# The last stage of a four-stage transformer kernel: who computes its gates, routing factors and roots, and in which order

## The reference, cut to what matters

```python
x = x + wkv(layernorm(x), ctx)              # stage 1
x = x + quantised_ffn(layernorm(x))         # stage 2
x = x + cross_attention(layernorm(x), ctx)  # stage 3: 8 groups x 2 heads
x = x + L1_ffn(layernorm(x))                # stage 4

def L1_ffn(x):                              # the sequence is the BATCH axis: l = 4 positions
    x = silu(x_prev * conv_w[:, 0] + x * conv_w[:, 1])
    q, k, v, g = silu(x @ Wq), x @ Wk, x @ Wv, x @ Wg       # 16 heads, 8 and 16 wide
    q, k = rotary(q), rotary(k)
    scores = softmax(v @ router_w)                          # 2 routes
    onehot = one_hot(argmax(scores))
    norm = 1 / cumsum(onehot over positions)
    qk = (q * scores * onehot * norm) . (k * onehot) * 8 ** -0.5, causal
    o = qk @ v
    o = (o - mean(o)) / sqrt(var(o) + 1e-5)                 # per head, 16 wide
    return (silu(g) * o) @ Wout
```

## Time and profile before

| | |
|---|---|
| median of 3 timed runs | 670.36 us (670.31 to 671.44) |
| the profiled execution's own time | 670.83 us |
| its span in the trace | 668.9 us |
| busy over the span | PE 92%, DVE 79%, ACT 60%, POOL 38% |
| mean granted TensorE clock | 0.987 of full |

### The profile page before, as it was taken

The page is one execution under the profiler, slowest core; times in us unless marked ns, Lnnn a source line. Parts: engine busy times, 40 slices in busy tenths (PEclk is TensorE's granted clock), DMA queues, the critical chain, the costliest instruction groups (busy, mean ns, idle before and its releaser), DMA issues.

```text
span 668.9 us, 13295 instructions
## 1 busy us (share of the span) xinstructions
PE 613.5 (92%) x4567; PEld 491.5 (73%) x4567; DVE 531.4 (79%) x1305; ACT 398.9 (60%) x1339; POOL 256.0 (38%) x338
## 2 busy tenths in 40 slices
PE   4556999999999999999999999999999999999937
PEld 3445787777778887778788877877888888767725
DVE  6998687988897778888877788888664777778797
ACT  4367766666776645667566456585663655655531
POOL 2215664444333454343335443333332444430233
PEclk9998999999999999999999999999999999999987
DMA  8475742424533202233342223332252323010001
GB/s 273 146 276 195 240 161 61 126 91 91 187 144 103 102 12 103 102 104 104 107 138 90 83 103 104 103 104 103 104 171 97 103 103 103 17 33 1 1 0 63
DMA packets 36973, 72.86 MB, mean 109 GB/s; under 512 B 3343, under 2 KB 28587, under 8 KB 32811
## 3 DMA queue, kind: packets, MB, share of 16 engines
q1 hardware_dynamic: 36720, 72.00, 32.9%
q10 hardware_dynamic: 186, 0.02, 0.0%
HBM read 59.41 MB, written 12.60 MB: 108 GB/s over the span
## 4 chain that ended last, share of the span: by engine, by line
PE 63%; DVE 21%; issue 7%; POOL 5%; ACT 4%; DMA 1%; SPq 0%; DVEq 0%; POOLq 0%
PE bank L718 13%; PE bank L698 11%; PE bank L587 10%; PE bank L594 6%; PE bank L670 5%; PE bank L742 3%; PE bank L684 3%; PE bank L699 3%; POOL rs L1351 2%; ACT square L1089 2%; DVE nm L1768 2%; DVE Cb L1783 2%; PE bank L834 2%; PE bank L732 1%; PE bank L843 1%
## 5 line engine op out<-in xcount | busy, mean ns | idle before, releaser
L718 PEld LDWEIGHTS bank<-V,Pt 128*128 128x128 f32 x1024 | 128.1, 191 | 29.1 <-DVE Cb L1783 15.3
L1089 ACT ACTIVATE square<-bank 128x128 bf16<-128x128 f32 x372 | 97.9, 280 | 85.0 <-PE bank L587 71.1
L718 PE MATMUL bank<-V,Pt 128*128 128x129 f32 x1024 | 136.3, 276 | 3.4 <-DVE Cb L1783 3.2
L698 PE MATMUL bank<-QT,KTt 128*128 128x512 f32 x256 | 132.6, 599 | 2.7 <-POOL diag L1366 2.7
L1366 POOL TENSOR_TENSOR diag<-identb,nm 128x512 bf16<-128x512 bf16 x64 | 66.9, 1045 | 173.3 <-DVE nm L1768 173.2
L1072 ACT ACTIVATE Pt<-bank 128x512 f32<-128x512 f32 x128 | 76.8, 600 | 65.4 <-PE bank L699 62.1
L1768 DVE TENSOR_REDUCE nm<-bank 128x2 f32<-128x512 f32 x128 | 82.4, 685 | 25.6 <-PE bank L684 25.2
L1351 POOL TENSOR_TENSOR rs<-ve,mhalf 128x6 f32<-128x6 f32 x64 | 90.0, 1406 | 5.3
L1783 DVE SCALAR_TENSOR_TENSOR Cb<-bank,ro,ism 128x128 bf16<-128x128 f32 x256 | 78.1, 347 | 4.5
L587 PE MATMUL bank<-WQ,xq 128*128 128x256 f32 x512 | 79.4, 297 | 1.5 <-DVE xq L1679 1.4
L1089 ACT ACTIVATION_READ_ACCUMULATOR square<-bank 128x1 f32 x372 | 78.0, 210 | 0.0
(11 more groups left out here) (233 smaller groups left out, 1021.1 us busy)
## 6 DMA issues: line engine op xcount, KB each, us to landing
WQ<-wq_split SPq DMA_DIRECT2D x24, 1024.0 KB, 7.7
WH<-wh_split SPq DMA_DIRECT2D x24, 384.0 KB, 8.9
wq_split<-WQ SPq DMA_DIRECT2D x8, 1024.0 KB, 5.4
ism<-smooth_inverse SPq DMA_DIRECT2D x32, 256.0 KB, 6.4
wpst<-in_L_xattn_wproj SPq DMA_DIRECT2D x16, 256.0 KB, 4.6
wh_split<-WH SPq DMA_DIRECT2D x8, 384.0 KB, 4.0
wst<-in_L_xattn_wq SPq DMA_DIRECT2D x8, 256.0 KB, 5.0
wst<-in_L_xattn_wqx SPq DMA_DIRECT2D x8, 256.0 KB, 5.2
```

Source lines behind the costliest of these rows:

```text
L698: nc.tensor.matmul(o[:], KTt[u % 2][:, x, t * P:(t + 1) * P], QT[u % 2][:, x, :], start=True, stop=False)
L718: last = nc.tensor.matmul(o[:, h * (P + 2):h * (P + 2) + P + 1], Pt[:, x, k, h * S + t * P:h * S + (t + 1) * P], V[u % 2][:, x, k, 0:P + 1 ...
L1089: last = A(square[:, t, h], head(t, h), ACT.Square, accum_out=ss[:, t, h:h + 1])
```

## The change

Everything is in the tail; the 31 units before it keep their code, apart from the products of three head groups of `project_last`, put into unit 30.

- **TensorE:** `project_last` goes by head groups. Group 0, then 1 and 2, of tile 0 move into unit 30; the transposes of inputs stand between the last `weigh`s. Tile 0 and tile 1 post `proj_done` each for itself. Keys and gates of a tile are separate steps with semaphores of their own (`qkv3_evac`, `g3_evac`); for the last two tiles the gates come first. PSUM banks are given out anew.
- **ACT:** `turned3` takes silu straight from PSUM for l = 0 and multiplies by the convolution's second weight for the others; hT is copied for l = 0 to 2 only. The tanh is taken beside the gate's evacuation, from PSUM (`gates3`). The roots take 1/16 and eps by scale and bias. A new `gate3(l)`, for l = 0 and 1, makes the gate product of a batch as 32 activations of 128 x 16, each with its own per-partition scale out of `r3`; both stand right behind the root over l = 0 to 2, ahead of turned 0, squares3(3), turned 1, the last root and turned 2.
- **DVE:** `convolve3` keeps one operation for each column half; `route3` makes the whole factor `wt` (routes, counts, score) before `dots3`, which multiplies once. `head_rstd3` moves ahead of the sum in `dots3(3)`. The tensor_scalar of `variance3` and `weigh3` of l = 0 to 2 go.
- **GpSimd:** it gets `weigh3(0)`, `(1)` and `(2)`, between the rotations; the rotation of l = 3 is done tile by tile (twelve operations instead of six); it keeps `gate3(2)` alone.

```diff
+        eps = sb("eps", [P, 1])
+            chain.add(gp.memset(eps[:], EPS))
...
                 weigh(u, 1, 1)
+                if u == UNITS - 2:
+                    project_last(0, (0,))
                 guard(u + 1, 1)
+                if u == UNITS - 2:
+                    project_last(0, (1, 2))
...
             weigh(u, 0, 1)
+            turn_inputs3(0)
             weigh(u, 1, 0)
+            turn_inputs3(1)
             weigh(u, 1, 1)
-            for l in range(B - 1):
-                turn_inputs3(l)
-            project_last(0, True)
+            turn_inputs3(2)
+            project_last(0, (3, 4, 5, 6))
+            project_last(1, (0, 1, 2, 3))
             turn_outputs(u)
-            project_last(1, True)
-            project_last(0, False)
-            project_last(1, False)
-            project3(0)
+            project_last(1, (4, 5, 6))
+            project_last(0, (7,))
+            project_last(1, (7,))
+            for m in range(NT):
+                project3_keys(m)
+                project3_gate(m)
             turn_inputs3(B - 1)
-            for l in range(1, B):
-                project3(l)
+            for m in range(NT, T8 - NT):
+                project3_keys(m)
+                project3_gate(m)
+            for m in range(T8 - NT, T8):
+                project3_gate(m)
+            for m in range(T8 - NT, T8):
+                project3_keys(m)
...
+            def gates3(m):
+                act.wait_ge(s["gate3_done"], m + 1)
+                l, t = divmod(m, NT)
+                B_ = P3B[m % 2]
+                A(dl[:, l, t * H3:(t + 1) * H3], B_[:, D:D + H3], ACT.Copy)
+                A(cf[:, l, t * H3:(t + 1) * H3], B_[:, D:D + H3], ACT.Tanh, scale=0.5)
+                A(g3[:, m, :], B_[:, 0:D], ACT.Silu).then_inc(s["g3_evac"], 1)
+
+            def gate3(l):
+
+                if l == 0:
+                    act.wait_ge(s["head_rstd_ready"], 1)
+                    act.wait_ge(s["og_ready"], B - 2)
+                for n in range(NT * H3):
+                    last = A(heads(o3, l)[:, n], heads(g3, l)[:, n], ACT.Copy, scale=r3[:, l, n:n + 1])
+                last.then_inc(s["o_ready"], 1)
...
             squares3(2)
             act.wait_ge(s["sd_ready"], B - 1)
-            A(r3[:, 0:B - 1], m3[:, 0:B - 1], ACT.Sqrt).then_inc(s["sd_done"], 1)
+            A(r3[:, 0:B - 1], m3[:, 0:B - 1], ACT.Sqrt, scale=1.0 / DV3, bias=eps[:]).then_inc(s["sd_done"], 1)
+            gate3(0)
+            gate3(1)
             turned_outputs3(0)
+            squares3(B - 1)
             turned_outputs3(1)
-            squares3(B - 1)
+            act.wait_ge(s["sd_ready"], B)
+            A(r3[:, B - 1], m3[:, B - 1], ACT.Sqrt, scale=1.0 / DV3, bias=eps[:]).then_inc(s["sd_done"], 1)
             turned_outputs3(2)
-            act.wait_ge(s["sd_ready"], B)
-            A(r3[:, B - 1], m3[:, B - 1], ACT.Sqrt).then_inc(s["sd_done"], 1)
...
+            def weigh3(l):
+
+                pool.wait_ge(s["sq_ready"], l + 1)
+                pool.wait_ge(s["g3_evac"], NT * (l + 1))
+                gp.tensor_tensor(rows3(g3, l), rows3(g3, l), rows3(o3, l), ALU.mult).then_inc(s["og_ready"], 1)
...
             power3(B - 1, B, 2)
-            for l in range(1, B):
-                rotate3(l)
-            for l in range(B - 1):
-                gate3(l)
+            weigh3(0)
+            rotate3(2, NT, 1)
+            rotate3(4, NT, 2)
+            weigh3(1)
+            rotate3(6, 1, 3)
+            rotate3(7, 1, 4)
+            weigh3(2)
+            gate3(2)
...
             def route3(l):
 
-                dve.wait_ge(s["qkv3_evac"], 3 * NT * (l + 1))
...
+                dve.wait_ge(s["g3_evac"], NT * m)
+                ch.add(v.tensor_scalar(sel[:, l], dl[:, l], 0.0, None, ALU.is_ge))
+                link(v.scalar_tensor_tensor(out=cf[:, l], in0=cf[:, l], scalar=-1.0, in1=cf[:, l], op0=ALU.mult, op1=ALU.max))
...
+                w = wt[:, 0:m, :]
+                link(v.tensor_tensor(w, sel[:, 0:m, :], sel[:, l:l + 1, :].to_broadcast([P, m, n3]), ALU.is_equal))
+                link(v.tensor_reduce(cnt[:], w.rearrange("p m n -> p n m"), AX_X, ALU.add))
+                link(v.reciprocal(cnt[:], cnt[:]))
...
             def dots3(l):
...
                 ch.add(v.tensor_tensor(pr.rearrange("p (m t c) -> p m t c", m=m, t=NT), k, q, ALU.mult))
...
                 if l == B - 1:
                     head_rstd3()
...
+                ch.wait()
+                link(v.tensor_reduce(lm[:, 0:m, :], pr.rearrange("p (m n d) -> p m n d", m=m, d=DK3), AX_X, ALU.add))
+                link(v.tensor_tensor(lm[:, 0:m, :], lm[:, 0:m, :], wt[:, 0:m, :], ALU.mult))
...
             convolve3(B - 1)
+            variance3(0)
             route3(1)
-            weigh3(0)
-            variance3(0)
             dots3(1)
             mix3(1)
             route3(2)
-            weigh3(1)
             variance3(1)
```

More of the change, by code:

```diff
@@ L181, in build_program @@
         lm = lb("lm", [P, B, NT * H3])
-        same = lb("same", [P, B, NT * H3])
+        wt = lb("wt", [P, B, NT * H3])
         cnt = lb("cnt", [P, NT * H3])
@@ L746, in project_out, with project_last @@
                     reader[XB.name] = (s["x3_ready"], b + 1)
[L748 to L759, removed]
+            def project_last(t, groups):
+                pe.wait_ge(s["catT_evac"], UNITS - G + groups[-1] + 1)
+                if t and groups[0] == 0:
+                    pe.wait_ge(s["qt_evac"], 4 * UNITS)
+                for g in groups:
+                    for f in (x * HEADS + g * HPG + h for x in range(2) for h in range(HPG)):
+                        last = nc.tensor.matmul(LAST_OUT[t][:, 0:D], catT[:, f, t * P:(t + 1) * P], WP[:, f, :],
+                                                start=f == 0, stop=f == CAT // P - 1)
+                if groups[-1] == G - 1:
                     last.then_inc(s["proj_done"], 1)
@@ L827, in project3 @@
                 wk = W3[:, :, K0:K0 + D // 2] if l == 0 else WK3[:, l - 1]
[L828 to L845, removed]
@@ new lines, in project3_keys @@
+                if m >= 2:
+                    pe.wait_ge(s["qkv3_evac"], 2 * (m - 1))
+                o = P3A[m % 2]
+                for k in range(KT):
+                    last = nc.tensor.matmul(o[:, 0:G0], cv[:, k, l, t * P:(t + 1) * P], W3[:, k, 0:G0], start=k == 0,
+                                            stop=k == KT - 1)
+                for k in range(KT):
+                    last = nc.tensor.matmul(o[:, G0:2 * D], cv[:, k, l, t * P:(t + 1) * P], wk[:, k], start=k == 0,
+                                            stop=k == KT - 1)
@@ new lines, in project3_keys, with project3_gate @@
+                last.then_inc(s["proj3_done"], 1)
+            def project3_gate(m):
+                l, t = divmod(m, NT)
+                if m >= 2:
+                    pe.wait_ge(s["g3_evac"], m - 1)
+                if t == 0:
+                    pe.wait_ge(s["silu_ready"], l + 1)
+                for k in range(KT):
+                    last = nc.tensor.matmul(P3B[m % 2][:, 0:K0 - G0], cv[:, k, l, t * P:(t + 1) * P], W3[:, k, G0:K0],
+                                            start=k == 0, stop=k == KT - 1)
+                last.then_inc(s["gate3_done"], 1)
@@ L1160, in turned3, with keys3 @@
                 act.wait_ge(s["h3T_done"], l + 1)
-                A(hT[:, :, l, :], T3B[l][:].rearrange("p (k t) -> p k t", k=KT), ACT.Copy).then_inc(s["h3T_evac"], 1)
+                x = T3B[l][:].rearrange("p (k t) -> p k t", k=KT)
+                for c in range(KT):
+                    last = A(cv[:, c, l, :], x[:, c], ACT.Copy if l else ACT.Silu, scale=vc(f"conv{c}", 1))
+                if l == 0:
+                    last.then_inc(s["silu_ready"], 1)
+                if l < B - 1:
+                    last = A(hT[:, :, l, :], x, ACT.Copy)
+                last.then_inc(s["h3T_evac"], 1)
             def silu3(l):
-                act.wait_ge(s["conv_ready"], l + 1)
+                act.wait_ge(s["conv_ready"], l)
                 A(cv[:, :, l, :], cv[:, :, l, :], ACT.Silu).then_inc(s["silu_ready"], 1)
-            def projected3(m):
-                act.wait_ge(s["proj3_done"], 2 * m + 1)
-                A_, B_ = P3A[m % 2], P3B[m % 2]
+            def keys3(m):
+                act.wait_ge(s["proj3_done"], m + 1)
+                A_ = P3A[m % 2]
                 qs = qkr[:, m, 0, :] if m < NT else q3[:, m, :]
@@ L1881, in convolve3 @@
                 for c in range(KT):
-                    now, before = vc(f"conv{c}", 1), vc(f"conv{c}", 0)
                     o = cv[:, c, l, :]
-                    last = v.tensor_scalar(o, hT[:, c, l, :], now, None, ALU.mult)
-                    if l:
-                        link(last)
-                        last = v.scalar_tensor_tensor(out=o, in0=hT[:, c, l - 1, :], scalar=before, in1=o, op0=ALU.mult,
-                                                      op1=ALU.add)
```

(5 more changed lines are left out.)

126 lines of the change are left out of this document (58 added, 68 removed).

## The result

The changed kernel takes 678.69 us (median of 4, 677.61 to 678.81) against 670.34 us of the kernel before: a ratio of 1.0119 with a 95% interval of 1.0107 to 1.0131, so 1.2% slower. The forecast was 676.9 us, in a range of 670.5 to 680.5. The profiled execution after took 678.73 us, with a span of 676.8 us.

What follows compares the result with a forecast made beforehand. Three limits in a row: TensorE's queue, DVE, then whoever releases TensorE's last queue. R 4.0 us earlier, second gate 10.1 later behind R, clock 0.5: span 6.6 more, 675.5; forecast 676.9 us, range 670.5 to 680.5.

Steps and rivals of the forecast that it cites:

- TensorE's queue: Tail up to the first projection: moved products and filled idle gaps bring it 1.7 us earlier, to 617.1.
- DVE up to R: DVE from route3(1) to R: 18.2 us plus 1.3 of GpSimd contention, so R at 648.5, 4 us earlier.
- R: The time at which head_rstd3, DVE's reciprocals for batches 0 to 2, ends: 652.50 us in the kernel before.
- the contention with GpSimd: DVE before R: 3 us more of GpSimd products, at 0.43 each, cost DVE 1.3 us; ends 0 and 2.6.
- DVE's gain is real: The forecast's closing claim: R comes 4.0 us earlier, but the gates eat that gain.
- The gates on ACT: Behind the reciprocals, 64 activations at 0.20 us take 12.8 us, putting the turn of batch 1 at 661.4.
- the low ends of 0.107 and 0.08: Lower prices in us per gate activation: from silus without a pointer, and from starts behind a 16-column PSUM copy.
- this rival: Pointers cost nothing: ACT's gates at 0.107 each take 6.85 us, time 671.0 us; chance 0.09.
- What queued behind: Behind ACT's gates: squares3(3) starts late, DVE idles before variance3(3), but the end follows the second ACT gate.
- From there: Turn of batch 1 to the span's end: 13.6 us as before, plus 0.5 for TensorE's low clock.
- GpSimd did not fall behind: Denies a rival: GpSimd's queue of weighs and rotations runs late, pushing R by 2 us, 678.9 us; chance 0.11.
- The rival that had ACT at hand-over pace: ACT's gate activations start every 0.08 us, 5.1 us in all, time 669.2 us; chance 0.07.

## Why the prediction was right, and where its sizes were off

**TensorE's queue.** Predicted first projection 617.1, measured 616.72, 2.1 us earlier than before where 1.7 were counted. The moved products and the filled gaps did it: the stretch from the first weigh to the first projection lost its idle time whole. The moved products found their cover in unit 30 too, where TensorE of the kernel before stood idle for 0.25 and 0.81 us (ahead of 599.02 and 600.74) and that of the changed one doesn't. The start of route3(1) was predicted at 629.0 and came at 629.19, but that closeness is luck: the first projection was 0.4 us early, and the first weigh on GpSimd made it 0.66 us late.

**DVE up to R.** Predicted 648.5, measured 649.94, within its ends of 646 and 650.5. The term that was mis-sized is the contention with GpSimd. It was set at 0.43 us of DVE for each us of GpSimd, from the long products beside the gates, 1.3 us in all, with a low end of 0 on the ground that the weighs fall beside sums. They fell beside small two-input operations, and these wait for GpSimd's whole product: 1.03 + 1.09 = 2.1 us. The trace of the kernel before already has such a case, which the prediction didn't use: beside GpSimd's first gate (653.03 to 654.09) a two-input operation took 1.03 us, and one of the same shape just ahead of the gate 0.28.

```profile
652.66 0.28 DVE L1918 TENSOR_TENSOR lm<-lm,same 128x128 f32<-128x128 f32 x1
...
653.20 1.03 DVE L1921 TENSOR_TENSOR lm<-lm,cnt 128x128 f32<-128x128 f32 x1
```

From route3(1) to R the forecast was 19.5 us and 20.74 were measured; 0.8 of the 1.2 us between them is this term, the other 0.4 isn't traced. Of the first weigh the prediction only asked whether it delays a rotation that DVE awaits; it held DVE's own convolve3(3) for 1.0 us. The run with the weighs on DVE prices both: from route3(1) to R 20.17 instead of 20.74 us, with two weighs of 0.69 more on DVE, and route3(1) itself 0.66 us earlier.

So "DVE's gain is real" was mostly wrong. From the first projection to R the kernel before took 33.69 us (618.81 to 652.50); the prediction had 31.4, and 33.21 were measured. Of 2.3 us that DVE's part was to save, 0.5 came; with the weighs on DVE it would have been 1.7 (31.98).

**The gates on ACT.** Predicted 12.8 us at 0.20 each, measured 12.80. The row that was taken (L1013, pointer and memories right, columns wrong) with the slope of a column from two others was the right one; the low ends of 0.107 and 0.08 belong to activations without a pointer and out of PSUM. The run without pointers measured the first of them exactly, and this rival's 671.0 us as 672.5, with an R that came 1.4 us later than it assumed.

**What queued behind.** Predicted 661.4 for the turn of batch 1, measured 662.82, all of the difference from R. DVE's idle time ahead of variance3(3) was to be over 5 us and was 7.42; TensorE's second pause was to be 5 and was 5.21.

**From there.** Predicted 13.6 + 0.5, measured 13.98. The clock's low level (0.50) reached until 667.5, through the first output product and into turn 2, which took 0.75 us in the chain; in the chain of the kernel before it took 0.44:

```profile
659.72 0.44 PE bank L857 x4
```

**Sum.** Predicted span 675.5, measured 676.8, 1.3 us later, of which R is 1.4. The medians differ by 8.35 us where 6.6 were forecast. GpSimd did not fall behind: its last rotation ended at 644.5, DVE needed it at 648.05. The rival that had ACT at hand-over pace, the only one that ended faster, fell with the run without pointers. The forecast came out because its largest term, the gates on ACT, was priced right; the terms that were off are the smaller ones.

What the prediction didn't see is that ACT's new order costs too, once the gates are gone: squares3(3) ahead of turned 1 and the root ahead of turned 2 each hold one of TensorE's products for an input that DVE makes last. In the changed kernel both are covered by the gates.

## What to carry to other kernels

Price a move between engines by the number of instructions as well as by elements: one GpSimd product of 1.06 us became 32 activations of 0.20 us, because each of these activations carries the scale of one head and tile only, and the queue behind them paid for it. An engine that has idle time on average can still be the wrong place for work that stands at the one moment when everything waits for it. And a two-input product given to GpSimd can hold a two-input operation of DVE for its whole length; beside a sum it cost nothing here.

## What the runs showed of the hardware that was not expected

- In this kernel a small two-input operation of DVE that met a GpSimd product lasted until that product had ended: 1.29 us instead of 0.26, 1.38 instead of 0.29, and two convolution steps 1.88 instead of 0.87. Three separate collisions, each about one GpSimd product long, where a proportional slowdown was assumed.
- In the other direction DVE seems to hold GpSimd, though no run took them apart: the four half-size rotation products that lay beside DVE's long products took 2.63 us in all in the changed kernel, while the four of the tile ahead of them took 1.06.
- Keeping TensorE's clock up through the pause brought the first output products from 3.03 to 1.89 us and nothing to the time, as long as the last of them waited for turned 2. With turned 2 moved ahead the same products gave 0.6 us in the medians, which is within the noise.
